# A decoder kernel's last layer of experts: seven tiles of tokens sorted and one dense, with the owner loads and the closing norms rewritten

## The reference

```python
xt = x.reshape(-1, 128)
logits = xt @ Wg.T
topk_logits, topk_idx = jax.lax.top_k(logits, 2)
w = jax.nn.softmax(topk_logits, axis=-1)
gates = jnp.zeros((T, 8)).at[rows, topk_idx].add(w)
h = jax.nn.gelu(jnp.einsum('th,ehi->tei', xt, W1) + b1, approximate=False)   # 128 -> 512 for each expert
o = jnp.einsum('tei,eih->teh', h, W2) + b2
y = jnp.einsum('te,teh->th', gates, o)
x = _layernorm(x + y)
```

## Time and profile before

| | us |
|---|---|
| median of 3 runs (lowest, highest) | 856.6 (852.42, 858.76) |
| the profiled execution, its own time | 858.11 |
| its span, first to last instruction | 856.0 |
| mean granted clock of PE, as a share of full | 0.862 |
| busy in the span: PE, DVE, ACT, POOL | 703.6, 593.3, 459.9, 442.4 |

### The profile page before, as it was taken

One profiled execution on the slowest core, in us unless ns is written; L12 is line 12 of the kernel. 1 busy time (PEld: TensorE's weight loads), 2 busy tenths in 40 slices (PEclk: granted clock), 3 DMA queues, 4 the chain that ended last, 5 costly groups with the idle time before them and its releaser, 6 DMA issues.

```text
span 856.0 us, 21377 instructions
## 1 busy us (share of the span) xinstructions
PE 703.6 (82%) x7986; PEld 535.2 (63%) x7986; DVE 593.3 (69%) x1575; ACT 459.9 (54%) x1132; POOL 442.4 (52%) x595
## 2 busy tenths in 40 slices
PE   5997987899998997899976999849768999843980
PEld 2675753577776785677634777628655677632980
DVE  4656868979889954788668988435549789641644
ACT  2114646778787663887624765336437667321660
POOL 3118845767655732344327876134566666333552
PEclk9557987989999998999987999579979999755995
DMA  8009400000000000000009200040125570004012
GB/s 331 4 0 286 57 2 0 2 1 2 1 2 1 2 2 0 2 3 3 3 1 234 64 3 3 2 96 32 41 82 177 163 209 3 2 22 99 33 38 77
DMA packets 50803, 44.66 MB, mean 52 GB/s; under 512 B 15408, under 2 KB 41136, under 8 KB 50192
## 3 DMA queue, kind: packets, MB, share of 16 engines
q1 hardware_dynamic: 48464, 38.70, 16.4%
q0 software_dynamic: 2240, 4.60, 1.5%
HBM read 30.94 MB, written 12.36 MB: 51 GB/s over the span
## 4 chain that ended last, share of the span: by engine, by line
PE 54%; DVE 20%; POOL 8%; issue 7%; ACT 5%; DMA 3%; SPq 0%; DVEq 0%; POOLq 0%; ACTq 0%
PE bank L810 5%; PE bank L831 5%; PE bank L819 4%; PE bank L994 3%; PE bank L846 3%; PE bank L728 3%; PE bank L1052 2%; PE bank L1059 2%; PE bank L902 2%; DVE pairs L1566 2%; DVE pairs L1562 2%; POOL slots_x L1939 2%; PE bank L879 2%; DVE X L1455 2%; DVE sm L1513 1%
## 5 line engine op out<-in xcount | busy, mean ns | idle before, releaser
L1881 POOL TENSOR_TENSOR sm<-sm,mx 128x512 f32<-128x512 f32 x80 | 83.9, 1051 | 42.6 <-DVE mx L1516 42.1
L1852 POOL TENSOR_SCALAR veps<-mv 128x1 f32<-128x1 f32 x112 | 27.1, 242 | 118.8 <-DVE mv L1451 118.7
L1150 ACT COPY pT<-bank 128x512 f32<-128x512 f32 x112 | 65.4, 584 | 38.3 <-PE bank L819 37.0
L1145 ACT ACTIVATE pr<-sm 128x512 f32<-128x512 f32 x112 | 70.1, 632 | 24.9 <-POOL sm L1881 24.4
L819 PE MATMUL bank<-W,pr 128*128 128x128 f32 x448 | 72.6, 286 | 8.1 <-ACT pT L1150 6.5
L1876 POOL TENSOR_TENSOR pairs<-KS,quad 128x512 f32<-128x512 f32 x56 | 60.0, 1073 | 36.2 <-ACT KS L1127 36.1
L1853 POOL TENSOR_TENSOR rstd<-veps,W 128x1 f32<-128x1 f32 x112 | 65.2, 582 | 9.3
L810 PE MATMUL bank<-pairs,Q 64*128 64x256 f32 x448 | 67.7, 423 | 2.0 <-DVE sm L1513 1.0
L831 PEld LDWEIGHTS bank<-VX,pT 64*64 64x64 f32 x3584 | 60.1, 139 | 12.6 <-issue 6.8
L831 PE MATMUL bank<-VX,pT 64*64 64x9 f32 (+1 forms) x3584 | 65.2, 203 | 1.9 <-ACT pT L1150 1.2
L819 PEld LDWEIGHTS bank<-W,pr 128*128 128x128 f32 x448 | 51.2, 145 | 20.5 <-issue 11.4
(11 more groups left out here) (347 smaller groups left out, 1920.8 us busy)
## 6 DMA issues: line engine op xcount, KB each, us to landing
big<-gup SPq DMA_DIRECT2D x4, 1024.0 KB, 10.2
rel_scratch<-G SPq DMA_DIRECT2D x16, 256.0 KB, 2.7
W<-small SPq DMA_DIRECT2D x1, 3206.5 KB, 11.9
big<-early SPq DMA_DIRECT2D x2, 1557.0 KB, 8.4
slots_x<-zero SPq DMA_DIRECT2D x2, 1472.0 KB, 24.9
big<-down SPq DMA_DIRECT2D x8, 256.0 KB, 9.1
QM<-rel_scratch SPq DMA_DIRECT2D x16, 128.0 KB, 2.8
PM<-rel_scratch SPq DMA_DIRECT2D x16, 128.0 KB, 2.7
```

The costliest lines, as they stand in the source:

```text
L1145: act.activation(pr[:, u % 2, 4 * h:4 * h + 4, :, :].rearrange("p g b k -> p b g k"), sm[:, 2 * (u % 2) + h, :].rearrange("p (b g k) -> p ...
L1150: act.copy(pT[:, u % 2, 4 * h:4 * h + 4, :], bank[BK[f"tu{h}"]][:, :].rearrange("p (h n) -> p h n", h=4)).then_inc(pt_ready, 1)
L1881: tt(v, v, bc(mx[:, slot, :], [P, 8, S], 2), ALU.subtract).then_inc(pcentered, 1)
```

## The change

`SORTED` = 7. Only tiles 0 to 6 are sorted and sent; tile 7 goes through all eight experts densely.

- **Fewer blocks and rows.** BLOCKS3 is (2·7·128 + 8·127) // 128 = 21 and POOL sends 14 indirect DMAs.
- **Routing in two parts.** PE computes the logits of tiles 0 to 5 ahead of the transpose of tile 6, and tile 6 ahead of the transpose of tile 7. DVE chooses for tiles 0 to 6 inside the attention's program, behind the statistics of tile 7 and ahead of its normalization (`choose_two(slice(0, 7), 1)`), and for tile 7 only behind the owners (`choose_two(slice(7, 8), 2)`).
- **Dense tile.** While the rows travel, PE runs four ups (128 columns each, ping-pong over banks 4 and 5) and four downs for each of the eight experts, ACT takes four gelus for each, and DVE adds each expert's result with its gate. The gates' transposes and the second bias stand behind the third expert's ups. Then DVE and POOL do tile 7's closing norm, and it is stored.
- **ACT's order.** Both kinds of row copies come first, then the gelus of expert 0, then the exponential, then the other experts.
- **Owner loads.** Each `value_load` stands in `fetch(j)`, behind its wait.
- **Closing norms.** For tiles 0 to 3 and 4 to 6: DVE takes mean and variance of all, ACT makes 1/sqrt of the group by a logarithm and an exponential, and DVE and ACT apply it to alternate tiles. POOL has no part in it. The stores follow the same order, and the last piece has three tiles.

```diff
-BLOCKS3 = (2 * TOK + NE3 * (P - 1)) // P
+SORTED = 7
+ROWS3 = ((0, 4), (4, SORTED))
+BLOCKS3 = (2 * SORTED * P + NE3 * (P - 1)) // P
...
 (PE, in chain)
-                        if name in ("x2", "x3") and t == MT - 1:
-                            logits(*(("e2.r", NE2) if name == "x2" else ("e3.r", NE3)), range(MT - 1))
+                        if name == "x2" and t == MT - 1:
+                            logits("e2.r", NE2, range(MT - 1), True, False)
+                        if name == "x3" and t == SORTED - 1:
+                            logits("e3.r", NE3, range(SORTED - 1), True, False)
+                        if name == "x3" and t == SORTED:
+                            logits("e3.r", NE3, range(SORTED - 1, SORTED), False, True)
...
 (PE, top2_ffn, behind the rank)
+                logits("e3.r", NE3, range(SORTED, MT), True, True)
+                wide = (MT - SORTED) * P
+                def all_up(e):
+                    if e == 0:
+                        pe.wait_ge(e3_in, 16 * 12)
+                    for c in range(4):
+                        mm(fill(4 + c % 2, h3_ready)[:, 0:wide], tile(e3_w[:, e, :], c), XT[:, SORTED * P:], start=True,
+                           stop=True).then_inc(h3_full, 1)
+                def all_down(e):
+                    pe.wait_ge(h3_ready, 4 * e + 4)
+                    ps = fill(2 + e % 2, row_added)
+                    for t in range(MT - SORTED):
+                        for c in range(4):
+                            last = mm(tile(ps, t), tile(HD[e % 2][:, c, :], t), tile(e3_w[:, e, :], 4 + c), start=(c == 0), stop=(c == 3))
+                    last.then_inc(block_full, 1)
...
+                for e in range(NE3 + 1):
+                    if e < NE3:
+                        all_up(e)
+                    if e >= 1:
+                        all_down(e - 1)
+                    if e == 2:
+                        gate_rows()
+                        second_bias()
...
 (ACT, top2_ffn)
+                for e in range(NE3):
+                    all_gelus(e)
+                    if e == 0:
+                        act.wait_ge(lg_ready, 4)
+                        act.activation(col[:, 4, :], col[:, 3, :], ACT.Exp).then_inc(score_ready, 1)
+                    if e == 2:
+                        for hh in range(2):
+                            act.wait_ge(choice_full, hh + 1)
+                            act.copy(half(gT, hh), bank[hh][0:NE3, :]).then_inc(choice_ready, 1)
...
+                act.preload_act_table_set("natural_log_exp_and_others")
+                before = 13 * MT + MT - SORTED
+                for hh, (first, after) in enumerate(ROWS3):
+                    act.wait_ge(var_ready, before + hh + 1)
+                    inverse_roots(rstd[:, first:after, :], rstd[:, first:after, :]).then_inc(score_ready, 1)
+                    act.wait_ge(score_ready, 3 + hh)
+                    act.wait_ge(rstd_ready, before + hh + 1)
+                    for t in range(first + 1, after, 2):
+                        act.activation(X[:, t, :], total_y[:, t, :], ACT.Identity, bias=veps[:, t, :], scale=rstd[:, t, :]).then_inc(restored, 1)
...
 (DVE, top2_ffn, behind the second bias)
+                for e in range(NE3):
+                    dve.wait_ge(block_full, BLOCKS + e + 1)
+                    if e >= 1:
+                        dve.wait_ge(row_added, e)
+                    for t in rest:
+                        last = stt(total_y[:, t, :], tile(bank[2 + e % 2], t - SORTED), gate[:, t, e:e + 1], total_y[:, t, :], ALU.mult,
+                                   ALU.add)
+                    last.then_inc(row_added, 1)
+                dve.wait_ge(row_added, NE3)
+                for t in rest:
+                    own_norm_done(t)
+                    stats(total_y[:, t, :], t)
                 dve.wait_ge(slot_ready, 4)
-                start = [dve.value_load(owner[0:1, j:j + 1], min_val=0, max_val=(NE3 - 1) * WIDE3) for j in range(BLOCKS3)]
...
+                for t in rest:
+                    dve.wait_ge(rstd_ready, due(rstd_ready))
+                    finish(total_y[:, t, :], t)
+
                 def fetch(j):
                     if j >= 3:
-                        dve.wait_ge(block_full, BLOCKS + j - 2)
-                    dve.tensor_copy(b1s[:, j % 3, :], big[:, 2 * NF3:][:, bass.ds(start[j], 4)])
-                    dve.tensor_copy(staged_w[j % 3], big[:, bass.ds(start[j], 2 * NF3)]).then_inc(staged, 1)
+                        dve.wait_ge(block_full, BLOCKS + NE3 + j - 2)
+                    at = dve.value_load(owner[0:1, j:j + 1], min_val=0, max_val=(NE3 - 1) * WIDE3)
+                    dve.tensor_copy(b1s[:, j % 3, :], big[:, 2 * NF3:][:, bass.ds(at, 4)])
+                    dve.tensor_copy(staged_w[j % 3], big[:, bass.ds(at, 2 * NF3)]).then_inc(staged, 1)
...
 (DVE, closing norms, for each of the two groups)
+                    for t in range(first, after):
+                        link(dve.bn_stats(st[:, t, :], total_y[:, t, :]))
+                        last = dve.bn_aggr(mv[:, t, :], st[:, t, :])
+                    link(last)
+                    own = slice(first, after)
+                    ts(rstd[:, own, :], mv[:, own, 1:2], EPS, None, ALU.add).then_inc(var_ready, 1)
+                    dve.wait_ge(score_ready, 3 + hh)
+                    stt(veps[:, own, :], mv[:, own, 0:1], -1.0, rstd[:, own, :], ALU.mult, ALU.mult).then_inc(rstd_ready, 1)
+                    for t in range(first, after, 2):
+                        ts(X[:, t, :], total_y[:, t, :], mv[:, t, 0:1], rstd[:, t, :], ALU.subtract, ALU.mult).then_inc(x_ready, 1)
```

More of the change, by code:

```diff
@@ L486, in decoder @@
         XK = WO[:, :, :, :, :].rearrange("p a b c n -> p (a b c n)")[:, 0:MT * (P + 1)].rearrange("p (t n) -> p t n", t=MT)
+        HD = [G[:, 2 * i:2 * i + 2, :].rearrange("p a n -> p (a n)").rearrange("p (c n) -> p c n", c=4) for i in range(2)]
         H3 = [pairs[:, 1 + i, :] for i in range(3)]
@@ L1035, in top2_ffn @@
-                for hh in range(2):
-                    pe.wait_ge(choice_ready, hh + 1)
-                    ps = fill(hh, acc_ready)
-                    for t in range(NT):
-                        last = mm(tile(ps, t), tile(gT, NT * hh + t), w("e3.b2")[0:NE3, :], start=True, stop=True)
-                    last.then_inc(b2_full, 1)
+                logits("e3.r", NE3, range(SORTED, MT), True, True)
[6 more added lines that the diff above has]
+                           stop=True).then_inc(h3_full, 1)
@@ new lines, in all_down, with gate_rows @@
+                def all_down(e):
[5 more added lines that the diff above has]
+                    last.then_inc(block_full, 1)
+                def gate_rows():
+                    pe.wait_ge(one_ready, 5)
+                    for hh in range(2):
+                        ps = fill(hh, choice_ready)
+                        for t in range(NT):
+                            last = pe.transpose(ps[0:NE3, t * P:(t + 1) * P], gate[:, NT * hh + t, 0:NE3], ident)
+                        last.then_inc(choice_full, 1)
@@ new lines, in second_bias @@
+                def second_bias():
+                    for hh in range(2):
+                        pe.wait_ge(choice_ready, hh + 1)
+                        ps = fill(hh, acc_ready)
+                        for t in range(NT):
+                            last = mm(tile(ps, t), tile(gT, NT * hh + t), w("e3.b2")[0:NE3, :], start=True, stop=True)
+                        last.then_inc(b2_full, 1)
+                for e in range(NE3 + 1):
[6 more added lines that the diff above has]
+                        second_bias()
@@ new lines, in top2_ffn @@
+            def top2_ffn():
+                g8, one8, two8 = gate[:, :, 0:NE3], one[:, :, 0:NE3], one[:, :, NE3:2 * NE3]
+                wide3 = 2 * SORTED
+                turns = newrow[:, :, :].rearrange("p a b -> p (a b)")[:, 0:NE3 * wide3]
+                link(dve.memset(turns, 1.0))
+                dve.memset(turns.rearrange("p (e m) -> p e m", e=NE3)[:, :, 0:1], 0.0).then_inc(init_dve, 1)
+                ts(XK[:, 0:SORTED, P].bitcast(I32), XB_id[:, 0:SORTED, P].bitcast(I32), float(TOK + BLOCKS * P), None,
+                   ALU.add).then_inc(init_dve, 1)
@@ L1782, in top2_ffn @@
                 dve.wait_ge(acc_ready, 2)
-                def add_rows(hh, k):
-                    dve.wait_ge(rel_back[2 * hh + k], 32 * MB // 4 + 16)
-                    for t in range(NT * hh, NT * hh + NT):
-                        last = stt(total_y[:, t, :], back_rows[k][:, t, :], col[:, 5 + k, t:t + 1], total_y[:, t, :], ALU.mult, ALU.add)
-                    last.then_inc(row_added, 1)
-                    dve.wait_ge(row_added, 2 * hh + k + 1)
-                for k in range(2):
-                    add_rows(0, k)
@@ L1793, in top2_ffn @@
[L1793 to L1807 removed]
+                for t in rest:
+                    dve.wait_ge(x_ready, LAST_NORM - MT + t - SORTED + 1)
@@ new lines, in top2_ffn @@
```

(13 more changed lines are left out.)

156 lines of the change are left out of this document (78 added, 78 removed).

## The result

The changed kernel took 863.0 us (median of 20 runs) beside 853.8 for the kernel before (also of 20): ratio 1.0099, 95% interval 1.0072 to 1.0126. Predicted were 858.4, within 851 to 866.5. So the sign held, but the loss was 9 us instead of 2. What follows shows that the agreement with the range is partly luck: two things that the prediction did not contain, one of -4 us and one of +11, stood against each other.

A forecast was written before the change was run, and what follows sets the result against it. PE bounds most of the chain, but idles 16.77 us while rows travel, which dense work was to fill. Last down +2.55 us and closing norms -0.8 gave about +1.8, so 859.9 profiled and a median of 858.4; range 851 to 866.5.

The forecast's parts named there:

- the sign: Whole kernel: the change was predicted to make it slower, by about 1.8 us.
- The dense tile: Tile 7's dense work while rows travel: PE done at about 786.9, 5.5 us after the rows could be there; bounds 784.4 and 800.0.
- half-clock: Rival, dense work: clock stays at half throughout, tile 7 ends at 800.0, 13 us later, total 871.5; chance 0.06.
- hidden-wholly: Rival: dense work hides wholly, blocks start where the rows arrive, total 850.1, or some 847.7 with clock kept up; chance 0.10.
- the kind clock: Rival: PE at full clock from 764.7, tile 7 ends 2.5 us earlier, filling 2.4 shorter, total 853.5; chance 0.17.
- From there to the first up: Between tile 7's dense end and the blocks: DVE's normalization and first fetch leave PE idle 3.6 us; bounds 2.9 and 4.5.
- Filling: Start of the block pipe, first up to first down's end: 6.1 us with half clock again, 3.7 at full clock.
- The blocks: Block stage: 20 steps instead of 22, owner load added to DVE's step, 1.93 us each, 38.6 in all; bounds 1.875 and 2.3.
- DVE paces the blocks: Rival, block stage: copies wait for POOL's whole write, steps of 2.3 us, 7.4 us lost, total 865.8; chance 0.15.
- The last down: End of the block stage: last down ends at 835.2, 2.55 us later than before.
- Closing norms: After the last down: the new norms and stores gain 0.8 us; bounds 0 and 2.
- PE is the bound from 764.7 on: Dense stretch, expert 1's gelus onward: PE sets the time with 58 matmuls, gates and bias, done at about 786.9.

The follow-up runs named there:

- again: The changed kernel, unaltered, measured once more: 852.0 us, end 107.5 us behind the third attention's last projection instead of 118.5, without the stall.
- fetch_first: Changed kernel with the first three fetches ahead of the bias additions: end 111.7 us behind the third attention's last projection, against 117.3 unaltered in the same job.
- loads_spread2: Changed kernel with first three fetches ahead and other owner loads between the dense additions, measured again in another job: 844.6 us, ratio 0.9882 to the kernel before.
- loads_spread: As fetch_first, with the other owner loads between the dense additions: mean block step 1.873 us instead of 1.928, end 0.5 us earlier.
- norms_only: Kernel before with only the new closing norms, in two halves of four tiles: 0.5% less in the medians, 3.5 us less behind the same last down.
- job 2: One set of kernels measured together on one chip, without the stall: changed kernel 852.0 us beside 853.5 for the kernel before.
- jobs 2 and 4: The two sets, each on its own chip, without the stall: unaltered changed kernel 852.0 us in the first, loads_spread2 844.6 us in the second.
- jobs 1, 3 and 5: The three sets with the stall: unaltered changed kernel 863.0 and 860.8 us in the first two; in the last, gates and second bias one expert earlier, dense part ending at 49.0.
- job 3: One set measured together on one chip, with the stall: unaltered changed kernel 860.8 us beside 856.2 for the kernel before.
- pool_last: norms_only with one tiny GpSimd memset behind VectorE's last normalization: 22.7 us from last down to end, against 19.9 without it.

## Why the prediction was right, and where not

Its times become distances from Y by taking 746.50 off. Against again, the execution without the stall:

- *The dense tile.* Predicted end 786.9, that is Y + 40.4; measured 783.35 + 1.95 - 745.11 = 40.2. The clock was to rise at 769.8, Y + 23.3; it rose at Y + 23.2, worked out from the mean of 0.67 in the window 765 to 770 of again, which has half clock ahead of it and full clock behind. The half-clock and the hidden-wholly rivals fall with it, and so does the kind clock's start at 764.7.

```profile
765.00:770.00 5.00, 4.88 (x28) 4.14 (x27) 0.00 (x0) 1.89 (x5) 3.78 (x5) 0.67 0.16 53
785.00:788.00 3.00, 0.41 (x4) 0.17 (x2) 1.25 (x5) 0.27 (x1) 0.79 (x2) 1.00 0.01 3
788.00:790.00 2.00, 0.69 (x3) 0.73 (x4) 1.55 (x4) 0.00 (x0) 0.00 (x0) 0.70 0.12 33
```

- *From there to the first up.* Predicted 3.6, measured 789.30 - 785.30 = 4.0. The profile puts the 3.90 us to "issue", but the up begins 0.1 us behind the end of VectorE's copy of the first expert's weights (788.51 + 0.69), as predicted. The pause costs the clock: the granted clock is 1.00 until 788 and 0.70 in 788 to 790. fetch_first confirmed both: with the fetches ahead, the pause and the fall of the clock are gone.
- *Filling.* Predicted 6.1, measured 794.00 + 1.83 - 789.30 = 6.5.
- *The blocks.* Predicted 20 steps of 1.93; measured 38.3 us, 1.915 each, and in the trace of loads_spread2 1.873 without the loads: 0.042 a step. Between fetch_first and loads_spread it is the predicted 0.055. The large copy takes 0.72 in the mean now, against a median of 0.76 in the earlier trace rows:

```profile
L1870 DVE COPY cap<-big 128x1024 f32 x12 | 8.7, 724 | 0.1
L1869 DVE COPY b1s<-big 128x4 f32 x18 | 5.3, 294 | 20.6 <-PE bank L1106 20.0 <-issue 0.6
```

 VectorE still idles over 1 us a step, waiting for PE. The rival "DVE paces the blocks" is refuted: the step isn't 2.3 us. The Trainium skill, "SBUF — State Buffer", section "Who interferes with whom", says that such a copy and a GpSimd instruction hold a shared port pair exclusively, each for its whole length; by that every copy would wait for the whole of GpSimd's write. The prediction took the copies' lengthening for small and let it be. In the traces it has a rule, and the page is right in one half. Before:

```profile
810.09 0.96 POOL L1944 DMA_INDIRECT back_y<-pT,token_of  x1 [0.96 <-DVE pT L1775]
810.62 0.93 DVE L1771 COPY cap<-big 128x1024 f32 x1
812.01 1.31 POOL L1944 DMA_INDIRECT back_y<-pT,token_of  x1 [0.96 <-DVE pT L1775]
812.51 0.69 DVE L1771 COPY Q<-big 128x1024 f32 x1
```

 A copy that begins 0.52 us or more into a write is lengthened, and all 15 such copies of before end 0.49 to 0.50 us behind the write's end (811.05 and 811.55 here), wherever they began; so do the 13 of again. The three of before that begin 0.24 to 0.50 us into a write keep their 0.69 us, and then the write is the longer one and ends 0.12 us behind the copy (813.20 and 813.32 here); the two of again do the same, with 0.12 and 0.16. So the two do exclude each other, as the page says, but not for the whole of the write: only a last part of under half of its 0.96 us clashes, and so a copy loses at most 0.24 us, which VectorE's idle time of over 1 us a step takes up.
- *The last down* was to end 2.55 us later than before; it ended 89.0 - 86.2 = 2.9 later. Every term up to here was right within half a microsecond.
- *Closing norms: the step that failed.* "I take 0.8 us gained; bounds 0 and 2." It summed the arithmetic up to the last normalization, and there it was nearly right: 11.75 us before, 11.2 in norms_only (838.43 to 849.65). It never asked what ended the span. The last output landed at 851.9, and norms_only shows that the kernel can end 0.4 us behind that; before, it ended at 856.0. So 3.7 us were GpSimd's drain, which the change moves off the path and which the sum put at nothing. Measured from the last down to the end: 23.4 to 18.5 in again, that is -4.9, of which 3.7 are the drain and 1.2 the arithmetic and the stores; -3.5 in norms_only, where the last piece has four tiles and the arithmetic and the stores come to +0.2. Hence the changed kernel is 2.0 us *shorter* behind Y where nothing stalls, not 1.8 longer; the medians of job 2 say -1.5 us, with an interval that includes no change.
- *The stall: the step that was missing.* "PE is the bound from 764.7 on" took for granted that PE runs on beside the indirect DMAs. It did so in the profiles of jobs 2 and 4, and lost 11.1, 9.9 and 5.7 us up to the dense part's end in those of jobs 1, 3 and 5 (51.3, 50.1 and 49.0 against 40.2, 40.2 and 43.3). No row of before could show it: PE was idle there, 5.58 us busy of 20. The rivals priced slower clocks and ports, none an engine that is held up. 118.5 - 107.5 = 11.0 us of difference between two executions of one program is that stall, with the clock that it costs. So the loss of 9 us is +2.9, -4.9 and +11.0. In job 3 the medians say +4.6 and not the 7.8 of the profiles; the kernel before was itself slower there (856.2), and its like in pool_last lost 1.3 us, which is part of it. The rest stays open.

Shown: the stall comes in some jobs and not in others, with one program; the dense part has it only with the indirect DMAs beside it; it ends with their stretch and isn't tied to certain instructions; and in one profile it struck VectorE, while PE had no work. Open: what differs between the jobs (jobs 2 to 5 had a chip each, so chip and job can't be told apart here), what holds the engines up, and whether recording takes part, since the counts missing in the same stretches show that records were lost. The Trainium skill, "NOTIFIC — Programmer's Manual", section "When the ring fills", says that a full queue of records drops new ones by default, and can be set to hold its producer; the lost counts agree with the first, and no run here shows the second. Every time in this study comes with a recorded span, so no run here could tell.

## What to carry to other kernels

Follow the chain to the very last record before you price a closing stage: an engine that ends with a long drain should be out of work early, and taking sixteen tiny instructions off it (3.7 us) was worth more than the arithmetic and the stores (1.2). Work that is meant to fill a wait needs its successors' preparations ahead of it, not behind: the same dense tile lost 4 us of hand-over with the fetches last, and gained 5.7 with them first. Where one program gives two medians in two jobs, lay the traces over each other at an event just ahead of the changed part before believing either.

## What the hardware showed that I had not expected

- GpSimd's drain at the end lasts 5.9 to 7.0 us in all 14 profiles, also behind a single memset.
- In three jobs PE's results came up to 8 us behind their records, and in one of them VectorE's loads were held up, while indirect DMAs ran; in two jobs not. The medians of the unaltered kernel are 863.0, 852.0 and 860.8, those of the kernel before 853.8, 853.5 and 856.2 in the same jobs.
- VectorE's 128x1024 copy and GpSimd's indirect DMA instruction exclude each other, but only over the last half microsecond of the latter: the copy then ends 0.50 us behind it, or it ends 0.12 to 0.16 us behind the copy (before and again).
- An owner load costs about 0.6 us on VectorE in a row, but 0.04 to 0.055 us a step beside blocks that PE bounds.
